# Third decoder layer: order of ScalarE's and VectorE's work in the attention groups, and which semaphores the expert loop waits on

## The reference, cut to what matters

```python
ln1 = layer_norm(hidden) ; q, k, v = split(ln1 @ qkv_weight.T)      # 16 heads, 4 key/value heads of 32
attn = softmax(causal(q @ k.T * scale)) ; proj = (attn @ v) @ proj_weight.T
h1 = hidden + proj ; x = layer_norm(h1) ; logits = x @ router_weight
top_p, top_i = top_k(softmax(logits), 2)                            # 8 experts, 2 for each row
xt = rows of x sorted by expert, at most cap for each              # cap = 1120
fc2 = gelu(xt @ moe_w1) @ moe_w2                                    # 512 -> 1024 -> 512
out = layernorm(hidden + h1 + share-weighted fc2 rows)
```

## Time and profile before

| | us |
|---|---|
| median of 3 runs | 4965.6 (4958.51 to 4974.67) |
| the profiled execution | 4960.01 |
| its span, first to last instruction | 4957.8 |

### The profile page before, as it was taken

One profiled execution on the slowest core, in us unless ns is written; L12 is line 12 of the kernel. 1 busy time (PEld: TensorE's weight loads), 2 busy tenths in 40 slices (PEclk: granted clock), 3 DMA queues, 4 the chain that ended last, 5 costly groups with the idle time before them and its releaser, 6 DMA issues. The chain is left out here.

```text
span 4957.8 us, 73350 instructions
## 1 busy us (share of the span) xinstructions
PE 3525.4 (71%) x27204; PEld 2410.9 (49%) x27234; DVE 2535.3 (51%) x3545; ACT 1613.3 (33%) x2869; POOL 592.9 (12%) x352
## 2 busy tenths in 40 slices
PE   0398631149414999999999999858871698988990
PEld 0143421136203566666666666535540577777770
DVE  6766788889761444444444444447652222222325
ACT  0104229978201333333333333222220233333321
POOL 0000000000000222222222222200004000000004
PEclk9999755555566999999999999978885899999995
DMA  3120432223203010000100001031002322222207
GB/s 131 65 83 0 120 87 83 83 78 102 70 17 118 17 47 27 25 25 25 44 29 25 25 25 32 5 68 35 26 18 87 118 77 72 72 72 72 72 31 243
DMA packets 176505, 303.70 MB, mean 61 GB/s; under 512 B 76648, under 2 KB 76648, under 8 KB 172160
## 3 DMA queue, kind: packets, MB, share of 16 engines
q1 hardware_dynamic: 167296, 273.37, 17.6%
q0 software_dynamic: 8960, 26.58, 1.5%
HBM read 172.42 MB, written 100.93 MB: 55 GB/s over the span
## 5 line engine op out<-in xcount | busy, mean ns | idle before, releaser
L1409 DVE TENSOR_REDUCE arena<-psum 112x4 f32<-112x1504 f32 x256 | 441.4, 1724 | 769.0 <-PE psum L1239 768.9
L1153 POOL TENSOR_TENSOR arena<-arena 125x896 f32<-125x896 f32 x192 | 401.7, 2092 | 1255.4 <-ACT arena L1382 1255.4
L1382 ACT ACTIVATE arena<-psum 125x1792 f32<-125x1792 f32 x192 | 320.0, 1667 | 400.6 <-PE psum L1252 400.6
L559 PE MATMUL psum<-arena 64*112 64x224 bf16 x1024 | 127.2, 401 | 348.2 <-DVEq L668 261.5
L684 ACT ACTIVATE arena<-arena,scales 112x224 bf16<-112x224 int8 x512 | 286.0, 559 | 35.3 <-DVEq L669 35.2
L2149 PE MATMUL psum<-tokens_T_high,w_high 128*128 128x384 f32 (+1 forms) x768 | 259.4, 338 | 21.8 <-issue 10.9
L1239 PE MATMUL psum<-arena 32*112 32x376 f32 x2048 | 235.8, 530 | 53.9 <-ACT arena L1382 27.0
L559 PEld LDWEIGHTS psum<-arena 64*112 64x112 bf16 x1024 | 81.8, 200 | 393.8 <-DVEq L668 283.8
L2149 PE MATMUL psum<-w_high,gelu_T_high 128*128 128x512 f32 (+1 forms) x576 | 231.8, 402 | 46.8 <-DVE arena L2280 39.3
L421 PE MATMUL psum<-arena 128*128 128x512 bf16 x1104 | 251.5, 383 | 14.0 <-DVEq L473 8.2
L2228 ACT ACTIVATE arena<-psum 128x384 f32<-128x384 f32 (+1 forms) x192 | 92.6, 482 | 510.9 <-PE psum L2151 510.7
(11 more groups left out here) (313 smaller groups left out, 7613.2 us busy)
## 6 DMA issues: line engine op xcount, KB each, us to landing
arena<-L_ffn_moe_w SPq DMA_DIRECT2D x16, 2048.0 KB, 11.2
arena<-arena SPq DMA_DIRECT2D x32, 896.0 KB, 5.3
arena<-ctx SPq DMA_DIRECT2D x16, 1500.0 KB
rows_by_slot<-arena SPq DMA_DIRECT2D x1, 17920.0 KB, 49.3
arena<-x SPq DMA_DIRECT2D x2, 7168.0 KB, 22.4
arena<-x_after_attn SPq DMA_DIRECT2D x32, 448.0 KB, 15.3
dots_ints<-arena SPq DMA_DIRECT2D x16, 784.0 KB, 4.8
arena<-dots_ints SPq DMA_DIRECT2D x16, 784.0 KB, 5.6
```

What stands on the lines that cost most here:

```text
L559: last = PE.matmul(psum[0:HALF, 4 * (hg % 2) + j, half * NS:(half + 1) * NS], stage[at, u, h // 2, half * HALF:(half + 1) * HALF], stage[a ...
L1153: G.tensor_tensor(pair2[:, t, :, :], prob[:, t, :, 0:NS], prob[:, t, :, NS:2 * NS], ALU.add).then_inc(paired, 1)
L1382: S.activation(prob[:, t, :, :], score_psum(MC, 2 * NS), ACT.Exp, scale=SCALE2).then_inc(exp_done, 1)
L1409: return V.tensor_reduce(rmx[:, i // 2, i % 2, :], score_psum(HALF, HC), axis=AX.X, op=ALU.max).then_inc(r_free, 1)
```

## The change

In the attention part:

- ACT copies the X transposes before it takes the square root, not after it.
- POOL adds tile by tile (128x512), and each tile's consumer waits for its own tile.
- DVE's second norm is cut in two: the first half (`ln2_centred`, L1915) runs before `probabilities`, the second (`ln2_scaled`, L1918) after it, and `normed(g+2)` follows both. After the last group the first half runs before `inverse`.
- At the start group 0's rows are issued first and the first norm's weight and bias before the projection weight; the projection weight and the second norm's parameters get semaphores of their own; PE's first transposes wait for the qkv weight alone; `normed(0)` comes before `base_variances(1)` and `constants()`.

In the expert part:

- The second semaphores and PE's waits for its own matmuls are gone. ACT and SP wait on the counts of the matmuls (`f_mm`, `y_mm`, `t_mm`) themselves; the counts start with an offset.
- `y_moved` starts at 2, so y tile t waits for the copy of the same bank one block earlier.
- Tile 2 of the transposes runs between y tile 0 and y tile 1.
- SP's load of block b+1's rows waits for all transposes of block b, which is one block more than it asked for.

The diff, cut to its core (in the first part `wb2_in` and `p_in` are the new semaphores):

```diff
                 def _(sp):
+                    load_by_rows(sp, xr[:, 0, :, :], r2_d, 0, LG, x_in[0])
                     sp.dma_start(qkv_r, ...).then_inc(w_in, 16)
-                    load_by_rows(sp, xr[:, 0, :, :], r2_d, 0, LG, x_in[0])
-                    sp.dma_start(prj_r, ...).then_inc(w_in, 16)
                     for j, n in enumerate(("weight", "bias")):
                         sp.dma_start(wb1[:, j, :], ...).then_inc(wb_in, 16)
+                    sp.dma_start(prj_r, ...).then_inc(p_in, 16)
...
                     for g in range(NG3):
-                        pool.wait_ge(o_read, LG * (g + 1))
-                        G.tensor_tensor(xr[:, g % RING, :, :], xr[:, g % RING, :, :], raw[:, :, :], ALU.add).then_inc(base_done, 1)
+                        for t in range(LG):
+                            pool.wait_ge(o_read, g * LG + (t + 1))
+                            G.tensor_tensor(xr[:, g % RING, t, :], xr[:, g % RING, t, :], raw[:, t, :], ALU.add).then_inc(base_done, 1)
...
                     for n in range(WN):
                         weights(n)
+                    project(0)
                     deviations(1)
-                    project(0)
                     queries_keys_values(0)
                     for g in range(NG3):
-                        deviations(g + 2)
                         if g + 1 < NG3:
                             project(g + 1)
+                        deviations(g + 2)
...
                     base_variances(0)
                     dve.sem_inc(var_done, 1)
-                    constants()
+                    inverse(0)
+                    normed(0)
                     base_variances(1)
                     dve.sem_inc(var_done, 1)
-                    inverse(0)
-                    normed(0)
+                    constants()
...
                         inverse(g + 2)
+                        if g >= 1:
+                            ln2_centred(g - 1)
+                        probabilities(g)
+                        if g >= 1:
+                            ln2_scaled(g - 1)
                         if g + 2 < NG3:
                             normed(g + 2)
-                        probabilities(g)
-                        if g >= 1:
-                            ln2(g - 1)
...
                 def tokens(e, q, b, u):
 
-                    sp.wait_ge(x_read, b + 1)
+                    sp.wait_ge(t_mm, b * BT + BT)
...
-                def transposed(q, b, u):
-                    pe.wait_ge(g_in[u], two_count(b, u))
-                    for t in range(BT):
+                def transposed(q, b, u, tiles):
+                    if tiles[0] == 0:
+                        pe.wait_ge(g_in[u], two_count(b, u))
+                    for t in tiles:
...
-                    pe.wait_ge(t_mm, BT * b + BT)
-                    pe.sem_inc(x_read, 1)
...
-                    pe.wait_ge(f_mm, b * NF + NF)
-                    pe.sem_inc(f_done, 1)
-                    if q == BLOCKS - 1:
-                        pe.sem_inc(w1_used, 1)
                     if more:
-                        transposed((q + 1) % BLOCKS, b + 1, 1 - u)
+                        transposed((q + 1) % BLOCKS, b + 1, 1 - u, (0, 1))
                     for t in range(BT):
+                        if more and t == 1:
+                            transposed((q + 1) % BLOCKS, b + 1, 1 - u, (2,))
                         pe.wait_ge(y_moved, b * BT + t)
...
-                    pe.wait_ge(y_mm, BT * b + BT)
-                    pe.sem_inc(g_used, 1)
-                    if q == BLOCKS - 1:
-                        pe.sem_inc(w2_used, 1)
-                loop4(pe, lambda: transposed(0, 0, 0), body)
+
+                def first():
+                    pe.sem_inc(t_mm, BT)
+                    pe.sem_inc(y_mm, BT)
+                    transposed(0, 0, 0, range(BT))
+                loop4(pe, first, body)
...
-                    act.wait_ge(w1_used, e)
+                    if not (isinstance(e, int) and e == 0):
+                        act.wait_ge(f_mm, e * (BLOCKS * NF))
...
-                    act.wait_ge(w2_used, e)
+                    act.wait_ge(y_mm, e * (BLOCKS * BT) + BT)
...
                         if f == 0:
-                            act.wait_ge(g_used, b)
+                            act.wait_ge(y_mm, b * BT + BT)
...
                 def first():
+                    dve.sem_inc(y_moved, 2)
```

More of the change, by code:

```diff
@@ L2054, in decoder_kernel @@
         yr = sb("expert_rows", [P, 2, BT, D], F32, L4)
[L2056 removed]
+        with phase(nc, "mo", "w1", "w2", "h1", "h2", "r1", "r2", "g0", "g1", "tm", "th", "tr", "fm", "ge", "gh", "gr",
                    "ym", "yv", "s0", "s1") as (
[L2058 to L2059 removed]
+                w1_in, w2_in, w1_high, w2_high, w1_rest, w2_rest, g_in0, g_in1, t_mm, xT_high, xT_rest,
+                f_mm, gelu_done, g_high, g_rest, y_mm, y_moved, st0, st1), nc.Block() as block:
             g_in, stored = (g_in0, g_in1), (st0, st1)
@@ L2213, in high_x @@
                 def high_x(q, b):
-                    act.wait_ge(f_done, b)
+                    if not (isinstance(b, int) and b == 0):
+                        act.wait_ge(f_mm, b * NF)
                     for t in range(BT):
-                        act.wait_ge(t_mm, BT * b + t + 1)
+                        act.wait_ge(t_mm, b * BT + (t + 1 + BT))
                         S.copy(xTh[:, :, x_cols(q, t)], x_psum(t, tile_rows(q, t))).then_inc(xT_high, 1)
```

36 lines of the change are left out of this document (17 added, 19 removed).

## The result

| | us |
|---|---|
| changed kernel, median of 4 runs | 4758.32 (4754.72 to 4763.89) |
| the kernel before beside it, median of 4 | 4962.06 |
| ratio | 0.9593, 95% interval 0.958 to 0.9605 |
| profiled execution, its span | 4760.2, 4758.4 |

The account below looks back on a forecast made before the run. PE was taken to bound both parts. Attention gains 12 + 46 + 12.4 = 70.4 plus expert 99 made 169.4 off 4960.0, so 4790.6; with 5.6 for the median 4796, rounded to 4795 us, range 4776 to 4830.

Parts of the forecast that it names:

- the expert part, 99 us: Expert part: PE's listed standstills gone, 88.5 us, plus 16 for pipeline refills, less 5; taken as 99, bounds 84 and 105.
- the loop's turn: Expert part, where the hardware loop turns: "issue" waits, two of nearly 5 us, were to stay, so no gain.
- 0.17 x 94: Expert part: refilling PE's pipeline costs 0.17 us beyond the wait at each of 94 stops, 16 us gained on top.
- 5 us held back for 46 passages: Expert part: PE might pause about 0.1 us at each of 46 passages from transposes to products, so 5 us deducted.
- The bound of 105: Expert part: upper bound of the gain, 105 us, beside 99 taken and a lower bound of 84.
- Rival 2: Expert part: stops give back less, as PE pauses anyway or lacks instructions; gain 74 instead of 99, 4820 us; chance 0.12.
- rival 4: Expert part: the next block's rows come late from SP, making the kernel slower than before; chance 0.01.
- The start, 12 us: Attention start: `normed(0)` ends at 3294.3, plus 1.7 us for weight transposes and reordering; X transposes 12 us earlier, bounds 8 and 14.
- rival 3: Port rule, attention part: POOL's additions and reordering collide with DVE; start loses 2.3, seven groups 1.1 each; 4805 us; chance 0.07.
- Groups 1 to 4, 46 us: Attention groups 1 to 4: 49.4 us each instead of 61.1, from vanished waits and queries at higher clock; 46 taken, bound 26.
- rival 1: Attention groups 1 to 4: the clock falls anyway, so the gain is 26 instead of 46, 4815 us; chance 0.13.
- Groups 5, 6 and the end, 12.4: Last attention groups: 4.6 us in group 5, 4.2 in group 6, and the stall and root after the last; sum 12.4.

Follow-up runs that it names:

- the halves: Kernel before with only the attention part of the change: 4892.62 us, ratio 0.9865; with only the expert part: 4820.71 us, ratio 0.9717.

## Why the prediction was right and where it failed

**The mechanisms held.** PE set the end in both parts before and after, and DVE in the last attention group. L1855 at 0.20, `route` behind `values`, no wait for L2285 or for tile 2, 33.3 to 34.4 us a block: as written. That the halves add, and that nothing between them moved, fits the sum.

**The failed step: the expert part, 99 us.** Measured 136.4. The terms that failed are the loop's turn, put at nothing, and the price and the number of the stops.
1. *The turn.* "The waits put down to 'issue' where the loop turns stay." They did not. The two turns took 5.4 and 4.9 us before and 0.6 or less after, and the f part behind the first is shorter too (18.0 instead of 21.9 us). "Issue" gave 8.8 us and the two f parts 4.3 beyond what other f parts gained: 13 us in all, and the experiment with the one wait at the turn brings 10.8 of them back. The own wait and the issue gap beside it stood in the list as two rows, and I had not asked whether one made the other.
2. *The number of stops.* The sum has 0.17 x 94, and gives no reason for 94. The earlier trace rows lists 48 + 23 + 23 + 22 + 23 = 139 beyond the opening block, and the prediction itself speaks of six a block. The 45 left out are 7.6 us at its own price.
3. *The price of a stop.* I took 0.17 for refilling from the y tiles. Of the 136.4 us 88.5 are the listed waits, 13.1 the turn and 0.8 the opening block; 34 are left for the 139 stops, 0.25 each: 0.20 at the y tiles, 0.27 after the f part, 0.29 among the short transposes. That is 10 us more. The kernels with the own waits back (8.8 us listed, 27 lost) and with both waits for DVE back (0.27 a stop) bear it out.
4. *5 us held back for 46 passages.* PE passes from product to transpose in 0.18 us, its ordinary pace: nothing was due.

Measured by kind, the two waits for DVE are 94.6 us (74 by my terms) and the own waits 41.8 (31 by my terms, less the 5). The 94.6 hold 14 us of waiting that the earlier trace rows does not list, because it shows only with the own waits gone. The split of 3 is read off the lengths; no run has each kind of stop alone.

The bound of 105 failed with the same terms: without any gain at the turn it would still have been 123.

**Rival 2**, that the stops give back less, was wrong in sign; **rival 4**, late rows, did not show: no wait for their transfer after the opening block.

**The start, 12 us: 9.7.** That is at the scores of group 0 (64.7 against 55.0 us from the first transfer of rows); at the X transposes, where the 12 were forecast, it is 8.7, and the transposes are then 1 us shorter. The norm ended when I had put it; the step that failed is the 1.7 us between it and the X transposes, which took 5.2. The projection weight, now behind the norm's, landed 3.7 us later, and POOL's copies took 4.80 instead of 2.28 us. The latter is rival 3 at its place, and on ACT 2.5 of the 3.3 us come back. The Trainium skill ("SBUF — State Buffer", "Who interferes with whom") would have POOL held up by DVE's operations with two SBUF inputs, and the trace agrees as far as it goes: 4.80 beside `normed`, 2.40 with small operations beside, 2.19 on ACT. By it the start would gain 9.7. That the scores gain just this is luck: the late weight has its share in it, and the place is another. The rest of rival 3, 1.1 us a group, did not come.

**Groups 1 to 4, 46 us: 41.9.** The first of them took 49.4 as forecast, the others 51.05. This is part of rival 1: the clock was 0.93 over such a group. The waits went as worked out; the step that failed is the 1.7 us for queries at the higher clock. I had taken the queries from group 0 (14.00) and the logits from group 5 (3.71 us), but in that group 5 the queries took 15.70. Of the groups after, the first alone has both; in the next four the logits take 4.54 to 5.04. Without the 1.7 the rows of group 5 give 30.3 - 3.1 + 23.8 = 51.0, what was measured.

**Groups 5, 6 and the end, 12.4: 13.0,** in parts 3.1 and 9.9 where I had 4.6 and 7.8; group 0, not priced, gave 1.1 more. And the part edit by edit: addition with root 21.7, second norm 28.2, start 14.5 make 64.4 of 65.9. That this comes so near is partly chance, since the start undone costs 14.5 and the change's start gave 9.7.

**DVE's slack** was given as 1 us and is 4.75 in the group shown, since `out` comes later than I had it; so the addition by tile is worth little by itself.

## What to carry to other kernels

A wait of an engine for its own last instruction can be dear out of all proportion to its row in the list of waits, and dearest just ahead of a loop's jump: look whether an "issue" gap stands beside it, and price the two together. Price a stop from start to start in the very kind of instruction in which it stands, not from the wait. Count the stops of every kind before multiplying by that price. Take the lengths of neighbouring stretches from one and the same group: what the lower clock doesn't cost in one it may cost in the next. Where the granted clock falls once in a cycle, find which stretch pays, and put short operations there. When edits are undone one at a time, undo pairs too: two that take the same wait away each look worthless alone (0 and 0.2 us up to the last scores, against 15.1), and one that pays only behind another makes the other look huge (135.6 against 94.6 for both).

## What the runs showed of the hardware

- A wait of PE for its last matmul ahead of the loop's jump: gaps of 3.9 to 5.0 us of "issue" at each turn with it, 0.2 to 0.9 without; the same wait away from the jump, in three places, cost 1.0 us in all.
- A stop of PE cost 0.20 to 0.29 us beyond its wait, on the average of 139 stops 0.25.
- Four copies of 128x512 on GpSimd: 2.28 and 2.40 us with little beside them, 4.80 beside DVE's norm; on ScalarE beside the same norm 2.19. A DVE operation over four columns lasted 3.45 us beside GpSimd's addition of a whole group and 0.20 with the addition by tile.
- The granted clock: with PE never waiting longer than 0.83 us in a group it still fell from the logits on (128x8 each), 0.84 over logits and `out`; after a stop of 6.9 us in the expert part it was 0.79 over the next 7 us.
